# Two layers in one kernel on one core: other PSUM banks and another order for the next batch's x, keys, V and first scores

## What is computed

```python
# layer A: 16 heads, Q is the normed x itself (8 columns a head), causal
K, V = split(x @ Wk + bk, 16), split(x @ Wv + bv, 16)     # V: 32 columns a head
attn = softmax(einsum('bhqd,bhkd->bhqk', split(x, 16), K) + mask)
xA = x + gelu(merge(attn @ V)) @ Wf + bf
# layer F: 8 heads of 64, causal, 8 experts for values and for the output
q, k = heads(x @ w_q), heads(x @ w_k)
g = sigmoid(x @ w_gate); gm = one_hot(argmax(g)) * g
values = einsum('bhne,ehdk,bnd->bhnk', gm, value_experts, x)
attn = softmax(where(causal_mask, min, einsum('bhid,bhjd->bhij', q * SCALE, k)))
out = einsum('bhne,ehkd,bhnk->bhnd', gm, output_experts, attn @ values).sum(1)
```

## Time and profile before

| | us |
|---|---|
| median of 3 runs | 1306.97 (1305.66 to 1310.4) |
| the profiled execution | 1294.37, its span 1292.6 |
| PE busy | 1124.5 (87%), weight loads beside it 625.1 (48%) |
| ACT busy | 966.5 (75%) |
| DVE busy | 866.5 (67%) |
| POOL busy | 360.2 (28%) |
| mean granted TensorE clock | 0.971 of full |

### The profile page before, as it was taken

How to read it: one execution, slowest core, us unless ns; L and a number is a source line. 1 busy time by engine, 2 the same in 40 slices (tenths; PEclk the granted TensorE clock), 3 DMA queues, 4 the chain that set the end, 5 groups by cost and what they waited for, 6 DMA issues and landing times.

```text
span 1292.6 us, 19886 instructions
## 1 busy us (share of the span) xinstructions
PE 1124.5 (87%) x5720; PEld 625.1 (48%) x5720; DVE 866.5 (67%) x2691; ACT 966.5 (75%) x2663; POOL 360.2 (28%) x460
## 2 busy tenths in 40 slices
PE   2687898998889998899989989899888998889998
PEld 1125643466434654357443564346643475435753
DVE  4735866577664967758676586658776486775845
ACT  3885788857886778966888578886788677896660
POOL 1023313232132512333232331323213251233210
PEclk7588999999999999999999999999998999999999
DMA  6211141022300323003320214102330032300220
GB/s 191 67 67 37 48 116 37 4 66 81 91 13 7 80 86 81 2 15 71 98 70 2 52 47 117 37 4 66 83 93 10 4 83 86 82 3 8 70 50 25
DMA packets 43645, 72.72 MB, mean 56 GB/s; under 512 B 9664, under 2 KB 25408, under 8 KB 43216
## 3 DMA queue, kind: packets, MB, share of 16 engines
q1 hardware_dynamic: 38416, 54.67, 15.5%
q10 hardware_dynamic: 5120, 16.78, 5.1%
HBM read 45.34 MB, written 8.80 MB: 42 GB/s over the span
## 4 chain that ended last, share of the span: by engine, by line
PE 48%; ACT 26%; DVE 11%; issue 6%; DMA 3%; POOL 2%; SPq 1%; ACTq 1%; DVEq 0%; POOLq 0%
ACT masked L860 15%; PE ps_m L649 9%; PE ps_o L637 8%; ACT pt L929 8%; PE ps_exp L550 3%; PE ps_exp L462 3%; PE ps_max L550 3%; DVE masked L1217 3%; PE ps_exp L464 2%; PE ps_exp L463 2%; PE ps_max L746 2%; DVE pt L1379 2%; PE ps_m L462 2%; PE ps_exp L552 2%; PE ps_m L464 2%
## 5 line engine op out<-in xcount | busy, mean ns | idle before, releaser
L1217 DVE CUSTOM_DVE_ANT_0 masked<-ps_max,mask 128x512 f32<-128x512 f32 (+3 forms) x768 | 352.7, 486 | 194.1 <-PE ps_max L550 108.7
L860 ACT ACTIVATE masked<-masked,low 128x512 f32<-128x512 f32 (+3 forms) x768 | 422.8, 553 | 51.9 <-DVE low L1217 49.0
L929 ACT ACTIVATE pt<-ps_exp 128x384 f32<-128x384 f32 (+1 forms) x480 | 240.7, 520 | 73.8 <-PE ps_exp L550 32.8
L1090 POOL TENSOR_SCALAR_AFFINE_SELECT pt<-pt 128x512 f32<-128x512 f32 (+2 forms) x192 | 139.0, 724 | 535.5 <-ACT pt L929 535.5
L649 PE MATMUL ps_m<-at,oe_sb 128*128 128x512 f32 x416 | 214.9, 605 | 0.1
L637 PE MATMUL ps_o<-pt,val 128*32 128x128 f32 (+6 forms) x1536 | 180.3, 450 | 10.8 <-POOL pt L1090 10.7
L550 PE MATMUL ps_max<-s2k,s1q 72*128 72x512 bf16 (+3 forms) x512 | 131.5, 319 | 36.2 <-DVE low L1217 19.7
L860 ACT ACTIVATION_READ_ACCUMULATOR masked<-masked,low 128x1 f32 x768 | 146.3, 191 | 0.0
L1268 DVE TENSOR_TENSOR at<-osb,hots 128x512 f32<-128x512 f32 x166 | 119.0, 721 | 17.9 <-PE ps_m L649 17.9
L550 PE MATMUL ps_exp<-s1q,s2k 75*128 75x384 bf16 (+3 forms) x384 | 98.6, 311 | 32.2 <-ACT pt L929 30.5
L550 PEld LDWEIGHTS ps_max<-s2k,s1q 72*128 72x128 bf16 x512 | 45.9, 99 | 137.4 <-DVE low L1217 78.7
(11 more groups left out here) (172 smaller groups left out, 1931.4 us busy)
## 6 DMA issues: line engine op xcount, KB each, us to landing
hots<-hot_d ACTq DMA_DIRECT2D x64, 256.0 KB, 4.8
s1q<-parts_q SPq DMA_DIRECT2D x96, 96.0 KB
s2k<-parts_k SPq DMA_DIRECT2D x96, 96.0 KB
s1q<-pt SPq DMA_DIRECT2D x64, 128.0 KB, 2.3
s1k<-pt SPq DMA_DIRECT2D x64, 128.0 KB, 2.3
parts_q<-pt SPq DMA_DIRECT2D x24, 128.0 KB, 2.3
parts_k<-pt SPq DMA_DIRECT2D x24, 128.0 KB, 3.0
x_sb<-in_x SPq DMA_DIRECT2D x8, 256.0 KB, 2.8
```

What stands on the lines that cost most here:

```text
L860: last = nc.scalar.activation(e, e, ACT.Exp, bias=low[:, g % 2, c:c + 1], scale=-1.0, accum_out=den[:, g % 2, c:c + 1])
L929: nc.scalar.activation(pt[:, (n % 2) * 4 + j, 0:c1 - c0], score_bank(k, u)[:, c0:c1], ACT.Exp).then_inc(exp_done[k].sem, 1)
L1090: nc.gpsimd.affine_select(out=v, in_=v, compare_op=ALU.is_ge, fill=0.0, base=0, pattern=[[0, HG[k]], [0, m], [1, P]], channel_multiplier=- ...
L1217: last = v.tensor_tensor_reduce(out=masked[:, u % JUNK, c0:c0 + w], in0=src[:, c0:c0 + w], in1=mask[:, S - w:S], scale=-1.0, scalar=POS, o ...
```

## The change

- The next batch's x goes to ps_o1 (index 7), its keys to ps_o0 (6), and its four V units to ps_exp0, ps_exp1, ps_o0 and ps_m0 (2, 3, 6, 0), where all of these had shared ps_m0, and ps_exp0 and ps_exp1. `weigh` of F waits for these banks' readers.
- The next x is transposed behind value unit 28 and no longer ahead of attention F; ACT and DVE take their parts of it in another order. The transposition of F's maxima of group 0 and its copy move from value unit 25 to 27. DVE negates the maxima of group 1 ahead of attention F's first maximum.
- The first two score units and exponentials of layer A stand among the last maxima units of its group 2 (SCORES_AT).
- SP sends the keys of layer A's group 1 ahead of the maxima rows of F's group 3 (the rows of group 2 stay ahead of the keys of group 0).
- Of the last batch, 16 choices and 15 products run in attention F, and 17 products behind it; DVE does all these choices.

```diff
-BANK = {("F", "xT", 0): 0, ("F", "gate", 0): 4, ("F", "gmT", 0): 4, ("A", "xT", 0): 0, ("A", "K", 0): 0,
+BANK = {("F", "xT", 0): 0, ("F", "gate", 0): 4, ("F", "gmT", 0): 4, ("A", "xT", 0): 7, ("A", "K", 0): 6,
...
-BANK.update({("A", "V", t): 2 + t % 2 for t in range(T)})
+BANK.update({("A", "V", t): (2, 3, 6, 0)[t] for t in range(T)})
...
-NEGATE_AT, TRANSPOSE_AT, COPY_AT = 23, 25, 25
+NEGATE_AT, TRANSPOSE_AT, COPY_AT = 23, 27, 27
...
+SCORES_AT = 10
...
-NEXT_AT = 7
+NEXT_AT, NEXT_X_AT = 7, 28
...
+OUTPUTS_LAST = {("F", u): [] for u in range(UNITS["F"])}
+for m in range(2 * E):
+    OUTPUTS_LAST["F", (14 + m // 2) if m < E else (18 + 3 * (m - E) // 4)].append(m)
...
                     restack_q(g)
-                    if g < 2:
-                        maxima_rows("F", f, 2 + g)
                     if g == 0:
+                        maxima_rows("F", f, 2)
                         sp.wait_ge(parts_out["k"].sem, parts_out["k"].count(f + 1, 16 * PARTS))
                     restack_k(g)
+                    if g == 1:
+                        maxima_rows("F", f, 3)
...
+                    pe.wait_ge(sums_out["F"].sem, sums_out["F"].count(a - 1, 3))
...
+                    if n == NEXT_X_AT and f + 1 < B:
+                        transposed("A", f + 1)
...
+                        if b + 1 < B:
+                            pe.wait_ge(kf.sem, kf.count(b + 1, 1))
                     else:
                         pe.wait_ge(gelu_done.sem, gelu_done.count(b, 1 + T))
+                        if b + 1 < B:
+                            pe.wait_ge(q_r.sem, q_r.count(b + 1, 1))
+                            pe.wait_ge(xl_done["A"].sem, xl_done["A"].count(b + 1, 1))
...
+                        if g == 2 and n == SCORES_AT:
+                            rows_arrived(a, 0)
+                            score_unit("A", a, 0, 0, 0)
+                            score_unit("A", a, 0, 0, 1)
...
             def attention_f(f):
-                if f + 1 < B:
-                    transposed("A", f + 1)
...
-            for u in range(E - 1, T * E):
+            for u in range(2 * E - 1, T * E):
                 product(B - 1, u)
...
                 if k == "F":
-                    logs(k, b, 1)
...
                     if b + 1 < B:
                         q_part0(b + 1)
+                    logs(k, b, 1)
+                    if b + 1 < B:
+                        act.wait_ge(moe1_ready.sem, moe1_ready.count(b, T * E))
+                        x_high("A", b + 1)
...
             def attention_f(f):
                 if f + 1 < B:
+                    x_low("A", f + 1)
                     q_rest(f + 1)
+                negate("F", f, 1)
...
-                            if m == 1 and g + 1 < GROUPS:
+                            if m == 1 and 1 <= g and g + 1 < GROUPS:
                                 negate("F", f, g + 1)
```

More of the change, by code:

```diff
@@ L241, in build @@
         ps_o = [bank("ps_o0"), bank("ps_o1")]
-        ps_m = [bank("ps_m0"), bank("ps_m1")] + ps_exp + ps_max
+        ps_m = [bank("ps_m0"), bank("ps_m1")] + ps_exp + ps_max + ps_o
         def score_bank(k, u):
@@ L457, in _ @@
             mm = nc.tensor.matmul
-            banks = [None] * 6
+            banks = [None] * 8
             def mm3(dst, lh, ll, rh, rl):
@@ L651, in outputs @@
             def outputs(f, phase, n):
-                for u in OUTPUTS[phase, n]:
+                for u in placed(f)[phase, n]:
                     if u >= 1:
@@ L662, in outputs_end, with rows_arrived @@
                 last.then_inc(out_ready.sem, 1)
+            def rows_arrived(a, g):
+                pe.wait_ge(mrow["A"][g % 2].sem, mrow["A"][g % 2].count(a, 16 * MROWS["A"] * (g // 2 + 1)))
             def attention_a(a):
@@ L676, in attention_a @@
                 for g in range(GROUPS):
-                    pe.wait_ge(mrow["A"][g % 2].sem, mrow["A"][g % 2].count(a, 16 * MROWS["A"] * (g // 2 + 1)))
+                    if g > 0:
+                        rows_arrived(a, g)
                     for s in range(STAGES):
@@ L681, in attention_a @@
                             u = n * HG["A"] + j
-                            score_unit("A", a, g, s, j)
+                            if u >= 2:
+                                score_unit("A", a, g, s, j)
                             if u in LATE:
@@ L807, in q_part0 @@
                 copy(part(0), ps_m[BANK[("A", "xT", 0)]][:]).then_inc(q1.sem, 1)
-                x_high("A", a)
             def q_part1(a):
@@ L896, in values_a, with weights @@
                     copy(val[:, t], ps_m[BANK[("A", "V", t)]][:]).then_inc(vb.sem, 1)
+            def weights(k, b, n, j):
+                u, s = n * HG[k] + j, n % STAGES
+                if j == 0:
+                    if n >= 2:
+                        act.wait_ge(pv_done[k].sem, pv_done[k].count(b, n - 1))
+                    elif k == "A":
+                        if pv_done["F"].count(b, 0):
+                            act.wait_ge(pv_done["F"].sem, pv_done["F"].count(b, 0))
+                    else:
+                        act.wait_ge(pv_done["A"].sem, pv_done["A"].count(b, NST))
+                act.wait_ge(s_ready[k].sem, s_ready[k].count(b, u + 1))
+                c0, c1 = ((0, S), (0, 384), (P, S))[s]
+                nc.scalar.activation(pt[:, (n % 2) * 4 + j, 0:c1 - c0], score_bank(k, u)[:, c0:c1],
+                                     ACT.Exp).then_inc(exp_done[k].sem, 1)
             def attention(k, b):
@@ L903, in attention @@
                     for n in range(n_units):
+                        if g == 2 and n == SCORES_AT:
+                            weights(k, b, 0, 0)
+                            weights(k, b, 0, 1)
                         denominators(k, b, g, n)
@@ L917, in attention @@
                         n = g * STAGES + s
[L918 to L924 removed]
                         for j in range(HG[k]):
                             u, m = n * HG[k] + j, s * HG[k] + j
[L927 to L930 removed]
+                            if k == "F" or u >= 2:
+                                weights(k, b, n, j)
                             if k == "F" and s == 1 and j == 0 and g + 1 < GROUPS:
@@ L1042, in _ @@
             q_part0(0)
+            x_high("A", 0)
             q_part1(0)
@@ L1271, in outputs @@
             def outputs(f, phase, n):
-                for u in OUTPUTS[phase, n]:
-                    if u not in POOL_UNITS:
+                for u in placed(f)[phase, n]:
+                    if u not in POOL_UNITS or f + 1 == B:
                         choose(f, u)
@@ L1441, in _ @@
             low_half(1, wv_h, wv_l, gflat[:, 128:640])
+            x_low("A", 0)
             q_rest(0)
@@ L1454, in _ @@
                     values_a(b + 1)
-            for u in range(E, T * E):
+            for u in range(2 * E, T * E):
                 choose(B - 1, u)
```

15 lines of the change are left out of this document (2 added, 13 removed).

## The result

The changed kernel is slower: 1318.04 us (median of 10 runs, 1311.41 to 1323.54) against 1307.12 for the kernel before (10 runs, 1303.76 to 1310.4), a ratio of 1.009 with a 95% interval of 1.0068 to 1.0113. The profiled run took 1323.54, its span 1321.6. I had forecast 1304.4 and a range of 1292 to 1315. The profiled run is the longest of the ten, and the profiled run of before was shorter than all ten of its timed ones, so the spans of the two profiles lie 29.0 us apart where the medians lie 10.9: the profiles show where the time went, the medians how much.

What follows compares the result with a forecast made beforehand. No one engine sets the end; ScalarE is late at attention F's start. Seven batches of 0.5 - 0.47 give +0.2, tail -1.3, clock -1.5: -2.6 from 1307.0, so 1304.4 us, range 1292 to 1315.

Steps and rivals of the forecast that it cites:

- part 5: Layer A's first two score units and exps among the last maxima: 0 claimed, bounds -0.7 and +0.5 us.
- part 7: TensorE's clock at the start of attention F: one of two low stretches of 1.5 us goes, -1.5 us in all.
- part 2: Start of attention F: ScalarE is late, its denominator delayed by VectorE's new order; +0.5 us a batch, bounds -0.2 and +0.8.
- Part 1: End of the value units: later copy and four transposes end the last unit 0.7 us later, F's scores start +0.3.
- part 4: Next batch's values: the fourth V unit, in the maxima's bank, starts 0.47 us sooner a batch; bounds -0.5 and 0.
- Part 3: Layer A's group 1 keys sent ahead of F's group 3 maxima rows: 0 claimed, bounds -0.3 and +0.4 us.
- Part 6: Tail: eight products moved into the last attention F, partly into TensorE's idle time; -1.3 us, bounds -2.4 and 0.
- second rival: Slower side: a 1.7 us wait at value unit 28 lowers the clock in six of seven batches; 1314 us, chance .17.

## Why the prediction was wrong, step by step

**The step that failed is part 5**, layer A's first scores, which I valued at 0 with a bound of +0.5. As a statement on the order it holds: ACT's wait ahead of unit 8 stayed at 1.49 once the clock was kept up, and it was right that unit 8 stands behind unit 7 and neither is moved. What I left out is that the step changes where PE idles. I asked that question in part 7, with rows from the start of attention F, and did not put it to layer A, though PE's wait there and the low stretch at 982.9 stood in the profile of before. With nothing else changed, the early scores made the kernel before 0.88% slower, some 11.5 us, which is the whole of the measured change. In the profile layer A cost +18.0, 2.6 a batch, where part 7 had priced a low stretch at 1.5: those that it looked at last 3.4 us, and the ones in layer A of the changed kernel 3.4 to 10.2.

**The sum** without it would have been near: the changed kernel without the early scores has a ratio of 1.0015, some +2 us, for the -2.6 forecast. Part of that is luck: the cost in part 2 and the gain in part 7 were both too small, and the two errors go against each other. By its other terms:

- *Part 1*, +0.7 at the value units: 0.80 in the profile (43.26 for 42.46). The transposes took 0.44, as said; the copy behind the denominator 0.36 and not 0.25. The wait at unit 28 was 1.49, I had 1.7:

```profile
785.31 0.50 PE L476 MATMUL ps_m<-ve_h,xh 128*128 128x512 f32 x1 [1.49 <-ACT mt_f L828]
```

- *Part 2*, a net +0.5 for the end of the value units and the start of attention F together: too small by the time the fourth V unit starts, and the way to it is wrong. ACT's first denominator of group 2 came at 793.39 after a wait of 1.15, 4.65 behind the start of the last value unit's last matmul, where I had it earlier than the 4.07 of before. The first step of the negation took 1.04 and not 0.16, and a new gap of 0.91 opened at 793.41 on PE for a row maximum, which I had not seen coming. But ACT caught up: at the third transposition of maxima, before at 781.33 and 15.3 behind the last value unit, the changed kernel is

```profile
803.71 0.27 PE L609 MATMUL ps_m<-ident_sb,nm_f 128*16 128x128 f32 x1 [0.36 <-DVE nm_f L1291]
```

15.0 behind it, 0.3 less, and with 0.80 of part 1 that is +0.5 at this point. What gave way is the 1.41 ahead of 777.51: I took that for ACT's time, but the issue of the four transfers ran beside its other work, and the same exp waited 0.47, by the profile for PE (the last issue too ended just ahead of it, as before). The 0.3 doesn't last. PE next waits for group 2's rows and group 0's keys, and these waits grew from 0.54 to 0.91 a batch on average (batches without a low stretch in attention F). At the fourth V unit attention F is 0.44 shorter (51.15 for 51.59), which is part 4 alone, so parts 1 and 2 cost the full 0.8 of the value units.
- *Part 3*, keys ahead of rows at 0: no wait of PE showed at group 3's rows or group 1's keys in any batch of any kernel. The waits for group 2's rows ahead of unit 12 (0.2 to 1.8 us) aren't of its making: both profiles of before have them too, in three and four of seven batches, and the changed kernel in six.
- *Part 4*, the fourth V at -0.47: from the first to the fourth unit it was 817.22 - 813.39 = 3.83 and is 839.96 - 836.60 = 3.36, so -0.47, and the wait is for mt_a's copy.
- *Part 6*, the tail at -1.3: 65.87 for 66.84, -1.0.
- *Part 7*, -1.5, for the start of attention F, the only place that it looked at: the direction was right there, the size too small. It also read its row short: the stretch of 460.70 holds both gaps of part 2, not only the first. Both low stretches at the start of attention F went. In four profiled kernels with moved x one of 28 batches had a low stretch in attention F, 23 us behind its start, against 17 in 49 with x in its old place and those waits unfilled, 16 of them 5.8 to 6.5 us behind it, at the end of the two gaps of part 2. At 1.5 us each that is some 3 us a run, where the value units lost 6. The second rival's own place, unit 28, did not lower the clock: no low stretch began there in any of these 28 batches.

So the rival on the slower side had the right kind of mechanism and the wrong place. It named 1314 for new low stretches in six of seven batches; the measured time is 1318 with new ones in all seven. I had given it 0.17.

**The scale.** I compared with a profiled run whose head happened to be 8 us short, and added the 12.6 back as a constant; that was fair: ten runs of before gave 1307.12 where three had given 1306.97, and the second profile of before took 1306.4.

What stays open: why the clock falls every time with the early scores and in 9 of 42 batches without them. In all nine it fell 12.8 to 13.8 us behind the fourth V unit, behind the one wait of 1.4 to 1.5 and before that of 1.07, which begins 15 us behind it. With the early scores it fell 14.4 to 17.0 behind, in seven of the 21 batches before the 1.07 had begun, so behind 0.64 and 0.79 alone. The experiments show that filling the waits ends it; they do not separate the length of the waits from their distance and from the work between them, and no run filled one wait and not the others.

## What to carry to other kernels

When a change moves matmuls without adding any, write down where TensorE will idle afterwards, at every place and not only where the change means to help, and price a low stretch of the clock there: here 1.5 to 5 us each, against 0 for the order itself. Where the profile shows low stretches behind waits, a few unread matmuls in a free bank, sized to the wait, are a cheap test of the cause and were worth 0.4% on their own. Before explaining a difference between two profiled runs, profile the old kernel a second time: 8 of 29 us were there without any change.

## What the runs showed of the hardware

- In profiled runs of closely related kernels the clock rose to full in the head either at 72 us (three runs, head 107.5 to 108.2) or only at 95 to 105 us (eight runs, head 114.7 to 119.9); the kernel before did both. In two more runs the record of the clock begins too late to tell, with heads of 115.4 and 117.7.
- With the early scores in place the low clock came in 21 of 21 batches; ten matmuls of 512 columns that nobody reads took it to 0 of 21, and layer A from a mean of 61.2 to 58.7 us.
- At the lower level a product's two matmuls took 1.91 us instead of 1.02 to 1.12.
